# GRU and mixture-of-experts kernel: input projections begun ahead of the recurrence, preparation in another order, five low halves on GpSimd

## The chip, the cores and the metric

The kernel runs on one core of one Trainium2 chip. The metric is the device time of an execution in microseconds. The kernel before has a median of 913.2 us over 3 runs (912.21 to 913.89). TensorE, VectorE, ScalarE, GpSimd and SyncE run side by side, each through its own instructions in order, and wait for each other by semaphores. The profile calls them PE (matmuls) with PEld (weight loads), DVE, ACT, POOL and SP.

## The reference

A GRU is scanned over 128 time steps of 16 sequences of width 512 (here 4 batches of 512 tokens, laid out so that the kernel can treat them as blocks), and its states go through a layer of four experts of which each token takes two; the result is added to x. Cut to what matters:

```python
def cell(h, x):
    gi = x @ W_ih + b_ih
    gh = h @ W_hh + b_hh
    i_r, i_z, i_n = jnp.split(gi, 3, axis=-1)
    h_r, h_z, h_n = jnp.split(gh, 3, axis=-1)
    r = sigmoid(i_r + h_r); z = sigmoid(i_z + h_z)
    n = tanh(i_n + r * h_n)
    return (1 - z) * n + z * h
_, hs = lax.scan(cell, cond_2048, x)           # x: 4 x 512 tokens of width 512
logits = hs @ Wg + bg                          # 4 experts, top 2, softmax
for i in range(4):                             # each takes its 512 best tokens
    out[sel] += gelu(tok @ W1[i]) @ W2[i] * p
x + out
```

## The kernel before

The sequences are cut into 64 columns that are computed side by side. A run of 40 steps over these columns follows: `FIRST` = 24 steps that bring the start states near their values (the first `ROUGH` = 20 of them with 16-bit high halves of the state alone), then 16 steps whose states are kept. After that come the gate of the experts, the choice of tokens, and for each expert two products (L538 and L551).

**The input projection gi = x W_ih** (12 tiles of 128 outputs by 512 columns, for each of four chunks of x) is made in two ways. The first chunk's 12 tiles are 32-bit matmuls on TensorE (L351), made before the recurrence. A tile lands in one of four banks of PSUM (banks 4 to 7). ScalarE scales and keeps it (`keep_tile`, L594: L601 for the r and z gates' tiles 0 to 7, L604 for the n gate's tiles 8 to 11), writes the high half in 16 bits (L616, `rz_high`), and VectorE subtracts to get the low half (L965, `rz_low`). An r or z tile stays in a ring of three buffers `gi_full` (`GI_RING`, L53), so that tile t can be kept only when the low half of tile t-3 is made (semaphore `gi_low`, L600). The other three chunks are made of 16-bit products, 12 matmuls a tile, 432 in all (`fill`, L355, matmul L368). They are given out over the first 24 steps of the recurrence, 18 a step (`FILL_STEP`), in a rough step as 13, 2, 2 and 1 ahead of the four parts of the state product (L376); ScalarE keeps these tiles behind a step's own work and VectorE makes their two halves at its end (`between`, L1135: a cast L958 and a subtraction L965).

**Chunk borders.** At steps 8 and 16 TensorE waits for all r, z high halves of the chunk that begins (L398), at step 24 for all high and low halves (L435, L436). TensorE's injection of gi into the gates is L386.

**The preparation** also takes the largest absolute value of x, W_ih, W_hh on VectorE (L919, L923, L931, L985, L1009), has GpSimd spread each over the partitions (`partition_all_reduce`: L768, L771, L774), turns it into powers of two, and splits W_ih, W_hh and x into halves (ScalarE L580, L584, L591; VectorE L973, L979). GpSimd then does one tiny product (L777, `warm`), and from then on the products z h of each step (L786).

SyncE issues all large loads, x of the first chunk first (L287), then W_ih in thirds (L289), the next x, W_hh in four parts, the rest of x. The order of work on each engine is written out by hand.

Of the kernel before, what the change touches and what calls it, by code (L numbers as in the profile page):

```python
# [36 lines left out]
def gru_moe(nc, x, x_t, cond_t, w_ih, w_hh, b_ih, b_hh, wg, bg, w1, w2, hs_rows, out):  # L37
# [18 lines left out]
    with ExitStack() as ctx:  # L56
# [154 lines left out]
        S["wih_loaded"] = [sem(f"wih_loaded_{g}") for g in range(3)]  # L211
        S["whh_loaded"] = [sem(f"whh_loaded_{k}") for k in range(KD)]
# [32 lines left out]
        assert FILL_STEP * STEPS_C == GI_MMS  # L245
# [13 lines left out]

        def rz_count(t):  # L260

            return sum(m < 8 for _, m in TILES[:t])

        def split_by(i):

            return 12 + 3 * (i + (i % STEPS_C == STEPS_C - 1)) // 2
# [19 lines left out]
        def _(sp):  # L286
            sp.dma_start(x_first, x_t[:, CHUNK_ORDER[0], :, :]).then_inc(S["x_loaded"][0], 16)  # L287
            for g in range(3):
# [48 lines left out]
        def _(pe):  # L337

            def bank_free(t):

                if t >= 4:
                    pe.wait_ge(S["gi_kept"], t - 3)

            pe.wait_ge(S["x_loaded"][0], 16)
            for m in range(12):
# [4 lines left out]
                for k in range(KD):  # L350
                    mm = pe.matmul(ps[:, 4 + m % 4, :], wih_sb[:, k, m * P:(m + 1) * P], x_first[:, k, :],  # L351
# [3 lines left out]
            def fill(first, last):  # L355

                for n in range(first, last):
# [10 lines left out]
                    mm = pe.matmul(ps[:, 4 + tile % 4, :], wih_parts[:, w, k, m * P:(m + 1) * P],  # L368
# [24 lines left out]
            def gates_rough(src, i):  # L393
                n = FILL_STEP * i
# [28 lines left out]

            pe.wait_ge(S["diag_ready"], 1)
            pe.wait_ge(S["whh_high"], KD)
            for i in range(ROUGH):
                gates_rough(i % 2, i)
            pe.wait_ge(S["whh_ready"], WHH_PIECES)
            for i in range(ROUGH, FIRST + L):
                if i < FILLED:  # L430
                    fill(FILL_STEP * i, FILL_STEP * i + FILL_STEP)
# [41 lines left out]
            pe.wait_ge(S["turn_ready"], 1)  # L473
# [91 lines left out]
        def _(act):  # L565
# [28 lines left out]
            def keep_tile(t, q, sc, g_sc):  # L594
# [3 lines left out]
                if m < 8:  # L598
                    if rz_count(t) >= GI_RING:
                        act.wait_ge(S["gi_low"], rz_count(t) - GI_RING + 1)  # L600
                    act.activation(gi_full[:, rz_count(t) % GI_RING, :], ps[:, 4 + t % 4, :], ACT.Identity,  # L601
                                   bias=bias_gi[:, q, m:m + 1], scale=sc).then_inc(S["gi_kept"], 1)
                else:
                    act.activation(gi[:, c, m % 4, 2, :], ps[:, 4 + t % 4, :], ACT.Identity, bias=bsum_g[:, m:m + 1],  # L604
# [19 lines left out]
            for m in range(4):  # L624
                first_tile(m)
            wih_high(0)
            wih_high(1)
            first_tile(4)
            wih_high(2)
            first_tile(5)  # L630
            wih_high(3)
            for k in range(KD):
                x_high(0, k)
            first_tile(6)
            act.wait_ge(S["gates_known"], 1)
            whh_high(0)
            first_tile(7)
            whh_high(1)
            whh_high(2)
            first_tile(8)  # L640
# [815 lines left out]
```

## Time and profile before

| | us |
|---|---|
| median of 3 runs | 913.2 |
| the profiled execution | 913.26 |
| its span, first to last instruction | 911.5 |
| first rough step's gates begin | 65.7 |
| PE busy, share of the span | 810.2 (89%) |
| DVE busy | 634.6 (70%) |
| ACT busy | 414.3 (45%) |
| POOL busy | 178.2 (20%) |

Times inside the profile count from the span's start. A row of a timeline gives start, duration, engine, line, what it writes and reads, its shape, how many are merged, and in brackets how long its engine had been idle and what ended that. Rows of one engine overlap by some 0.05 to 0.1 us, so that the distance between starts is a little under the duration. The granted clock of TensorE is given as a share of its 2.4 GHz.

### The profile page before, as it was taken

The page shows a single profiled execution, that of the slowest core. Times are in us where ns is not written, and L with a number is a line of the kernel's source. Part 1 is how long each engine was busy: PE and PEld are TensorE (multiplying, and loading weights), DVE is VectorE, ACT ScalarE, POOL GpSimd, SP SyncE. Part 2 cuts the span into 40 slices and gives each one's busy share as a digit, 9 for nine tenths or more (in the row PEclk, how much of TensorE's full clock was granted, in tenths as well). Part 3 has the DMA queues.
Part 4 walks back from the last instruction along what each step waited for, and adds up shares of the span by engine and source line. Part 5 has one row for each costly group of instructions (what it writes and reads, how often), then busy time and mean ns, then how long its engine had stood idle before and what let it go on. Part 6 is the DMA issues. An engine that isn't in the chain of part 4 may idle for free.

```text
span 911.5 us, 28124 instructions
## 1 busy us (share of the span) xinstructions
PE 810.2 (89%) x11698; PEld 533.4 (59%) x11699; DVE 634.6 (70%) x2087; ACT 414.3 (45%) x852; POOL 178.2 (20%) x454
## 2 busy tenths in 40 slices
PE   5979899997999999999957145999999999999996
PEld 2436565576999899999947143444444444444442
DVE  6868989765888888888875666766775766774500
ACT  0747566543454454545434302834283347416600
POOL 1002212122333333433320001012102100110011
PEclk9989999998999999999987557999999999999999
DMA  9800000000000000000013561247143715360011
GB/s 343 304 0 2 2 1 3 2 3 3 4 5 4 4 4 5 4 4 4 4 29 160 147 223 47 97 136 208 24 138 94 212 16 186 69 193 12 1 24 23
DMA packets 20165, 62.57 MB, mean 69 GB/s; under 512 B 2064, under 2 KB 2064, under 8 KB 17424
## 3 DMA queue, kind: packets, MB, share of 16 engines
q1 hardware_dynamic: 15744, 52.46, 16.6%
q0 software_dynamic: 3584, 8.42, 5.2%
q8 instruction: 85, 1.39, 0.6%
q14 instruction: 32, 0.26, 0.1%
q10 hardware_dynamic: 720, 0.03, 0.1%
HBM read 52.49 MB, written 12.62 MB: 71 GB/s over the span
## 4 chain that ended last, share of the span: by engine, by line
PE 69%; DVE 20%; issue 4%; ACT 3%; DMA 1%; POOL 0%; DVEq 0%; ACTq 0%; POOLq 0%
PE ps L376 18%; PE ps L538 18%; PE ps L551 18%; PE ps L368 8%; DVE wa L1047 4%; DVE wa L1052 3%; DVE halves L1063 3%; ACT wa L648 2%; PE ps L480 2%; PE ps L386 2%; DVE ocand L1056 1%; PE ps L518 1%; PE ps L526 1%; DMA bg_sb<-in_bg 1%; DVE big L965 1%
## 5 line engine op out<-in xcount | busy, mean ns | idle before, releaser
L376 PE MATMUL ps<-halves,wa 128*128 128x64 f16 x8448 | 290.6, 194 | 7.9 <-DVE halves L1063 1.6
L376 PEld LDWEIGHTS ps<-halves,wa 128*128 128x128 f16 x8448 | 274.2, 98 | 35.4 <-DVE halves L1063 15.9
L538 PE MATMUL ps<-wb,big 128*128 128x512 f16 x768 | 166.9, 379 | 1.5 <-DVE wb L1351 1.5
L551 PE MATMUL ps<-big 128*128 128x512 f16 x768 | 166.9, 379 | 0.0
L648 ACT ACTIVATE wa<-ps,un_gates 128x128 f32<-128x128 f32 x288 | 100.1, 365 | 139.0 <-PE ps L376 132.5
L1047 DVE SCALAR_TENSOR_TENSOR wa<-ps,bhn_s,wa 128x64 f32<-128x64 f32 x288 | 80.2, 278 | 72.2 <-ACT wa L648 72.2
L538 PEld LDWEIGHTS ps<-wb,big 128*128 128x128 f16 x768 | 74.7, 98 | 91.5 <-issue 1.7
L551 PEld LDWEIGHTS ps<-big 128*128 128x128 f16 x768 | 75.2, 98 | 89.9
L653 ACT ACTIVATE wa<-wa,un_gates 128x64 f32<-128x64 f32 x288 | 99.1, 344 | 57.5 <-DVE wa L1052 51.1
L368 PE MATMUL ps<-hx,wb 128*128 128x512 f16 x432 | 109.7, 386 | 4.9 <-DVEq L1022 4.9
L713 ACT ACTIVATE hx<-ps,un_hid_in 128x512 f32<-128x512 f32 x64 | 43.7, 683 | 112.4 <-PE ps L538 112.4
L1063 DVE SCALAR_TENSOR_TENSOR halves<-ocand,neg_scale,wa 128x64 f16<-128x64 f32 (+1 forms) x288 | 86.8, 301 | 4.5 <-issue 0.5
L1243 DVE SCALAR_TENSOR_TENSOR big<-wa,scale,big 128x2048 f16<-128x2048 f32 x28 | 65.3, 2349 | 26.0 <-ACT big L699 26.0
L699 ACT ACTIVATE big<-wa,scale 128x2048 f16<-128x2048 f32 x32 | 62.5, 1988 | 44.6 <-DVEq L1231 44.6
L1364 DVE SCALAR_TENSOR_TENSOR big<-hx,hid_scale,big 128x512 f16<-128x512 f32 x64 | 47.9, 749 | 42.8 <-ACT big L716 41.4
L386 PE MATMUL ps<-big,diag 128*128 128x128 f16 x496 | 62.8, 221 | 10.9 <-DVE big L958 10.9
L1202 DVE TENSOR_REDUCE chunk_peak<-wa 128x1 f32<-128x2048 f32 x32 | 71.1, 2276 | 0.0
L1052 DVE TENSOR_TENSOR wa<-wa,big 128x64 f32<-128x64 f32 x288 | 66.0, 229 | 5.1
L1056 DVE SCALAR_TENSOR_TENSOR ocand<-wa 128x64 f32<-128x64 f32 x288 | 62.6, 217 | 0.1
L368 PEld LDWEIGHTS ps<-hx,wb 128*128 128x128 f16 x432 | 38.5, 99 | 40.8 <-DVEq L1022 5.7
L786 POOL TENSOR_TENSOR wa<-wa,hx 128x64 f32<-128x64 f32 x128 | 42.6, 333 | 78.7 <-ACT wa L648 73.9
L844 POOL DMA_INDIRECT out<-hx,idx_out x16 | 29.1, 1816 | 136.1 <-DVE hx L1370 136.1
(178 smaller groups left out, 686.2 us busy)
## 6 DMA issues: line engine op xcount, KB each, us to landing
wa<-in_w SPq DMA_DIRECT2D x32, 1024.0 KB, 5.9
hs_rows<-big SPq DMA_DIRECT2D x8, 516.0 KB, 6.2
big<-in_w_ih SPq DMA_DIRECT2D x3, 1024.0 KB, 11.4
hx<-in_x_t SPq DMA_DIRECT2D x3, 1024.0 KB, 20.2
big<-in_w_hh SPq DMA_DIRECT2D x4, 768.0 KB, 16.5
wa<-in_x_t SPq DMA_DIRECT2D x1, 1024.0 KB, 5.2
hx<-hs_rows,idx POOLq DMA_INDIRECT x16, 3.7
out<-hx,idx_out POOLq DMA_INDIRECT x16, 4.8
```

What stands on the lines that cost most here:

```text
L368: mm = pe.matmul(ps[:, 4 + tile % 4, :], wih_parts[:, w, k, m * P:(m + 1) * P], x_parts[:, q, t, k, :], start=(left == 0), stop=(left == K ...
L376: mm = pe.matmul(gate_ps[:, j, g, :], whh_parts[:, k, w, (4 * g + j) * P:(4 * g + j + 1) * P], halves[:, src, k, h, :], start=False, stop= ...
L386: pe.matmul(gate_ps[:, j, 0:2, :], diag[:, 1 if c in (1, 2) else 0, :], gi_rz[:, c, j, part, :, cols], start=(part == HIGH), stop=False, s ...
L538: mm = pe.matmul(ps[:, m % 2, :], w1p[:, w, k, m * P:(m + 1) * P], tokT[:, t, k, :], start=(k == 0 and n == 0), stop=(k == KD - 1 and n == 2))
L551: mm = pe.matmul(ps[:, 2 + g % 2, :], hid[:, h, k, g * P:(g + 1) * P], w2p[:, w, k, :], start=(k == 0 and n == 0), stop=(k == KH - 1 and n ...
L648: act.activation(rz[:, j, :, :], gate_ps[:, j, 0:2, :], ACT.Sigmoid, scale=un_gates[:, 0:1]).then_inc(S["sig_done"], 1)
L653: act.activation(cand[:, j, :], cand_in[:, j, :], ACT.Tanh, scale=un_gates[:, 0:1]).then_inc(S["tanh_done"], 1)
L1047: dve.scalar_tensor_tensor(rn[:, j, :], gate_ps[:, j, 2, :], bhn_s[:, j:j + 1], rz[:, j, 0, :], ALU.add, ALU.mult).then_inc(S["rn_done"], 1)
L1052: dve.tensor_tensor(cand_in[:, j, :], rn[:, j, :], gi_n(j), ALU.add).then_inc(S["candin_ready"], 1)
L1056: dve.scalar_tensor_tensor(ocand[:, j, :], rz[:, j, 1, :], -1.0, cand[:, j, :], ALU.add, ALU.mult).then_inc(S["ocand_done"], 1)
L1063: dve.scalar_tensor_tensor(high_of(j), old(ocand_, j), neg_scale[:, 0:1], old(zh_, j), ALU.mult, ALU.add).then_inc(S["high_ready"], 1)
L1202: dve.tensor_reduce(chunk_peak[:, c:c + 1], stage[:, c * CHUNK:(c + 1) * CHUNK], AX.X, ALU.max, apply_absolute_value=True).then_inc(S["chu ...
```

## The change

Five things are edited.

- **Fills ahead.** The first 24 of the 432 fill matmuls (`PREFILL`, two tiles) are issued before the recurrence; the steps then take 18 each from number 24 on, until all are given out, so that step 22 has 12 and step 23 none. ScalarE keeps a tile once the first 13 fills of the next step can have made it (`kept_by`), and VectorE makes the halves one step later (`split_by`).
- **Banks.** The first chunk's 12 tiles use all eight banks (`gi_bank`), so TensorE waits for a kept tile only from tile 8 on. As the recurrence uses banks 0 to 3, TensorE waits for `gi_kept` 12 before its first step.
- **Loads.** x of the first chunk and the first third of W_ih come in four pairs of pieces, and the first four tiles are made piece by piece.
- **Order.** VectorE takes the biases after the maxima, takes the four maxima of W_hh in a row, and moves the splits of W_ih and x behind the scales of the gates; ScalarE keeps three tiles, splits W_ih and x, and then alternates the other r, z tiles with W_hh.
- **GpSimd.** It makes the four copies of the identity into `turn` (as products) and the low halves of tiles 3 to 7. These stand behind its three `partition_all_reduce` and the `warm` product, and wait for `gi_low` 3, that is for VectorE's low halves of tiles 0 to 2.

GpSimd's order in the preparation, before (`peak_all` is what it spreads, `warm` the tiny product, `ISA` rows without a tile carry no data):

```order
L768 ISA
L768 ISA peak_all<-peak 128x3 [waits peak_ready]
L771 ISA peak_all<-peak 128x2 [waits peak_ready]
L774 ISA peak_all<-peak 128x1 [waits peak_ready]
L777 ISA
L777 TENSOR_TENSOR warm<-ones 128x1 [waits consts_dve]
L786 TENSOR_TENSOR wa<-wa,halves 128x64 [waits sig_done] x80
```

The same place after (`big<-gi_full,big` are the low halves):

```order
L795 ISA
L795 ISA peak_all<-peak 128x3 [waits peak_ready]
L798 ISA peak_all<-peak 128x2 [waits peak_ready]
L801 ISA peak_all<-peak 128x1 [waits peak_ready]
L804 ISA
L804 TENSOR_TENSOR warm<-ones 128x1 [waits consts_dve]
L806 TENSOR_TENSOR turn<-ident 128x128 x4
L810 TENSOR_TENSOR big<-gi_full,big 128x512 [waits gi_high,gi_low]
L810 TENSOR_TENSOR big<-gi_full,big 128x512 [waits gi_high] x4
L821 TENSOR_TENSOR wa<-wa,halves 128x64 [waits sig_done] x80
```

Nine products now stand between `warm` and the first product of the recurrence.

ScalarE's order from the first tile that needs GpSimd's low halves to the recurrence, after (L627 keeps a tile in the ring, L642 writes its high half, L610 is W_hh's high half, L630 keeps an n tile):

```order
L610 ACTIVATE wa<-big,scale 128x1536 [waits gates_known]
L627 ACTIVATE gi_full<-ps,bias_gi,gi_scale 128x512 [waits gi_low,gi_mm]
L642 ACTIVATE big<-gi_full 128x512 [waits gi_kept]
L610 ACTIVATE wa<-big,scale 128x1536
L627 ACTIVATE gi_full<-ps,bias_gi,gi_scale 128x512 [waits gi_low,gi_mm]
L642 ACTIVATE big<-gi_full 128x512 [waits gi_kept]
L610 ACTIVATE wa<-big,scale 128x1536
L627 ACTIVATE gi_full<-ps,bias_gi,gi_scale 128x512 [waits gi_low,gi_mm]
L642 ACTIVATE big<-gi_full 128x512 [waits gi_kept]
L610 ACTIVATE wa<-big,scale 128x1536
L630 ACTIVATE big<-ps,bsum_g,gates_scale 128x512 [waits gi_mm] x4
```

These are tiles 5, 6 and 7, each followed by a part of W_hh, and then the four n tiles; before, tile 6 stood ahead of the first part of W_hh and tile 7 behind it.

TensorE at the start of the recurrence, after:

```order
L392 MATMUL ps<-hx,wb 128x512 [waits gi_kept,x_split,wih_split]
L392 MATMUL ps<-hx,wb 128x512 x11
L392 MATMUL ps<-hx,wb 128x512 [waits gi_kept]
L392 MATMUL ps<-hx,wb 128x512 x11
L392 MATMUL ps<-hx,wb 128x512 [waits gi_kept,whh_high,diag_ready]
L392 MATMUL ps<-hx,wb 128x512 x11
L392 MATMUL ps<-hx,wb 128x512 [waits gi_kept]
L410 MATMUL ps<-big,diag 128x128 [waits rn_done,high_ready,gi_high]
```

Two tiles of 12 fills stand ahead of the wait for W_hh and `diag`, where before there was none.

The diff, without the parts in which only a bank's name changes:

```diff
S["wih_loaded"] = [sem(f"wih_loaded_{g}") for g in range(3)]
+        S["first_loaded"] = [sem(f"first_loaded_{k}") for k in range(KD)]
         S["whh_loaded"] = [sem(f"whh_loaded_{k}") for k in range(KD)]
...
         GI_MMS = 12 * KD * 3
-        assert FILL_STEP * STEPS_C == GI_MMS
+        PREFILL = 24
+        assert FILL_STEP * STEPS_C == GI_MMS and PREFILL % (3 * KD) == 0
+
+        def filled(i):
+
+            return min(PREFILL + FILL_STEP * i, 3 * GI_MMS)
...
+        def gi_bank(t):
+
+            return t % 8 if t < 12 else 4 + t % 4
+
         def rz_count(t):
...
+        def kept_by(i):
+
+            return 12 + (PREFILL if i < 0 else min(filled(i) + FILLS[0], 3 * GI_MMS)) // (3 * KD)
+
         def split_by(i):
-            return 12 + 3 * (i + (i % STEPS_C == STEPS_C - 1)) // 2
+            return kept_by(i - 1) if i >= 0 else 12
+        assert split_by(STEPS_C - 1) >= 24 and split_by(2 * STEPS_C - 1) >= 36 and split_by(FILLED - 1) == 48
+        assert kept_by(2 * STEPS_C - 1) <= 38
...
         def _(sp):
-            sp.dma_start(x_first, x_t[:, CHUNK_ORDER[0], :, :]).then_inc(S["x_loaded"][0], 16)
-            for g in range(3):
+            for k in range(KD):
+                sp.dma_start(x_first[:, k, :], x_t[:, CHUNK_ORDER[0], k, :]).then_inc(S["first_loaded"][k], 16)
+                sp.dma_start(wih_sb[:, k, 0:D], wih_src[:, k, 0:D]).then_inc(S["first_loaded"][k], 16)
+            for g in range(1, 3):
                 sp.dma_start(wih_sb[:, :, g * D:(g + 1) * D], wih_src[:, :, g * D:(g + 1) * D]
...
-                if t >= 4:
-                    pe.wait_ge(S["gi_kept"], t - 3)
-
-            pe.wait_ge(S["x_loaded"][0], 16)
-            for m in range(12):
+                if t >= 8:
+                    pe.wait_ge(S["gi_kept"], t - 7 if t < 16 else t - 3)
+
+            for k in range(KD):
+                pe.wait_ge(S["first_loaded"][k], 32)
+                for m in range(4):
+                    mm = pe.matmul(ps[:, gi_bank(m), :], wih_sb[:, k, m * P:(m + 1) * P], x_first[:, k, :],
+                                   start=(k == 0), stop=(k == KD - 1))
+                    if k == KD - 1:
+                        mm.then_inc(S["gi_mm"], 1)
+            for m in range(4, 12):
...
                 for k in range(KD):
-                    mm = pe.matmul(ps[:, 4 + m % 4, :], wih_sb[:, k, m * P:(m + 1) * P], x_first[:, k, :],
+                    mm = pe.matmul(ps[:, gi_bank(m), :], wih_sb[:, k, m * P:(m + 1) * P], x_first[:, k, :],
                                    start=(k == 0), stop=(k == KD - 1))
...
                         bank_free(tile)
-                    mm = pe.matmul(ps[:, 4 + tile % 4, :], wih_parts[:, w, k, m * P:(m + 1) * P],
+                    mm = pe.matmul(ps[:, gi_bank(tile), :], wih_parts[:, w, k, m * P:(m + 1) * P],
                                    x_parts[:, q, t, k, :], start=(left == 0), stop=(left == KD * 3 - 1))
...
             def gates_rough(src, i):
-                n = FILL_STEP * i
+                n = filled(i)
                 for k in range(KD):
...
+            fill(0, PREFILL)
             pe.wait_ge(S["diag_ready"], 1)
             pe.wait_ge(S["whh_high"], KD)
+            pe.wait_ge(S["gi_kept"], 12)
             for i in range(ROUGH):
...
                 if i < FILLED:
-                    fill(FILL_STEP * i, FILL_STEP * i + FILL_STEP)
+                    fill(filled(i), filled(i + 1))
                 if i == ROUGH:
...
-            pe.wait_ge(S["turn_ready"], 1)
+            pe.wait_ge(S["turn_ready"], KD + 1)
             for n in range(NT):
...
                         act.wait_ge(S["gi_low"], rz_count(t) - GI_RING + 1)
                                    bias=bias_gi[:, q, m:m + 1], scale=sc).then_inc(S["gi_kept"], 1)
                 else:
                                    scale=g_sc).then_inc(S["gi_kept"], 1)
...
             act.wait_ge(S["x_known"], 1)
-            for m in range(4):
+            for m in range(3):
                 first_tile(m)
-            wih_high(0)
-            wih_high(1)
-            first_tile(4)
-            wih_high(2)
-            first_tile(5)
-            wih_high(3)
+            for k in range(KD):
+                wih_high(k)
+            act.wait_ge(S["x_loaded"][1], 16)
             for k in range(KD):
                 x_high(0, k)
-            first_tile(6)
+            first_tile(3)
+            first_tile(4)
             act.wait_ge(S["gates_known"], 1)
             whh_high(0)
+            first_tile(5)
+            whh_high(1)
+            first_tile(6)
+            whh_high(2)
             first_tile(7)
-            whh_high(1)
-            whh_high(2)
-            first_tile(8)
             whh_high(3)
-            for m in range(9, 12):
+            for m in range(8, 12):
                 first_tile(m)
...
             act.wait_ge(S["gi_known"], 1)
+            for t in range(12, kept_by(-1)):
+                tile(t)
             for i in range(FIRST + L):
...
                     continue
-                for t in range(12 + 3 * i // 2, 12 + 3 * (i + 1) // 2):
+                for t in range(kept_by(i - 1), kept_by(i)):
                     tile(t)
...
             pool.tensor_tensor(warm[:, :], ones[:, 0:1], ones[:, 0:1], ALU.mult).then_inc(S["warmed"], 1)
+            for k in range(KD):
+                pool.tensor_tensor(turn[:, k, 0:P], ident[:, :], ident[:, :], ALU.mult).then_inc(S["turn_ready"], 1)
+            pool.wait_ge(S["gi_low"], 3)
+            for t in range(3, 8):
+                pool.wait_ge(S["gi_high"], t + 1)
+                pool.tensor_tensor(gi_rz[:, CHUNK_ORDER[0], t % 4, LOW, t // 4, :], gi_full[:, t % GI_RING, :],
+                                   gi_rz[:, CHUNK_ORDER[0], t % 4, HIGH, t // 4, :], ALU.subtract
+                                   ).then_inc(S["gi_low"], 1)
...
             dve.wait_ge(S["steps_made"], 1)
-            dve.wait_ge(S["small_loaded"], 16 * 5)
-            dve.tensor_tensor(bsum[:, 0:8], bih[:, 0:8], bhh[:, 0:8], ALU.add)
-            dve.tensor_copy(bsum[:, 8:12], bih[:, 8:12]).then_inc(S["bias_ready"], 1)
-            dve.wait_ge(S["bias_ready"], 1)
-            dve.tensor_reduce(peak[:, BIAS:BIAS + 1], bsum[:, 0:8], AX.X, ALU.max, apply_absolute_value=True)
...
-            dve.wait_ge(S["x_loaded"][0], 16)
+            for k in range(KD):
+                dve.wait_ge(S["first_loaded"][k], 32)
             dve.tensor_reduce(chunk_peak[:, 3:4], x_first, AX.XY, ALU.max, apply_absolute_value=True
...
             for g in range(3):
-                dve.wait_ge(S["wih_loaded"][g], 16)
+                if g > 0:
+                    dve.wait_ge(S["wih_loaded"][g], 16)
                 dve.tensor_reduce(chunk_peak[:, g:g + 1], wih_sb[:, :, g * D:(g + 1) * D], AX.XY, ALU.max,
...
             link_n[0] += 4
-            dve.wait_ge(S["consts_pool"], 1)
-            for k in range(KD):
-                dve.tensor_copy(turn[:, k, 0:P], ident[:, :])
+            dve.wait_ge(S["small_loaded"], 16 * 5)
+            dve.tensor_tensor(bsum[:, 0:8], bih[:, 0:8], bhh[:, 0:8], ALU.add)
+            dve.tensor_copy(bsum[:, 8:12], bih[:, 8:12]).then_inc(S["bias_ready"], 1)
+            dve.wait_ge(S["bias_ready"], 1)
+            dve.tensor_reduce(peak[:, BIAS:BIAS + 1], bsum[:, 0:8], AX.X, ALU.max, apply_absolute_value=True)
             dve.tensor_copy(turn[:, :, P:P + E], wg_sb[:, :, :]).then_inc(S["turn_ready"], 1)
...
-            for m in range(4):
-                rz_low(m)
-
             def wih_low(k):
...
                 ins = dve.tensor_reduce(chunk_peak[:, k:k + 1], whh_sb[:, k, :], AX.X, ALU.max, apply_absolute_value=True)
-                if k < KD - 1:
-                    wih_low(k)
-                if k in (1, 2):
-                    rz_low(3 + k)
             link(ins)
...
             dve.sem_inc(S["peak_ready"], 1)
-            wih_low(KD - 1)
-            rz_low(6)
+            rz_low(0)
+            dve.wait_ge(S["consts_pool"], 1)
             dve.wait_ge(S["peak_known"], 2)
...
             dve.sem_inc(S["gates_known"], 1)
-            for k in range(KD):
-                x_low((0, k))
-            rz_low(7)
+            wih_low(0)
+            rz_low(1)
             for n in range(2, NC_):
...
             dve.sem_inc(S["peak_ready"], 1)
+            wih_low(1)
+            rz_low(2)
+            wih_low(2)
+            wih_low(3)
+            for k in range(KD):
+                x_low((0, k))
             dve.wait_ge(S["peak_known"], 3)
...
             dve.sem_inc(S["gi_known"], 1)
+            dve.wait_ge(S["gi_low"], 8)
...
```

## Rows read from the trace of the kernel before

**Rows 1.** Timeline of the preparation, VectorE (columns as told above).
```profile
11.43 0.17 DVE L893 TENSOR_TENSOR bsum<-bih,bhh 128x8 f32<-128x8 f32 x1 [7.58 <-DMA bg_sb<-in_bg]
...
20.56 0.62 DVE L928 COPY turn<-ident 128x128 f32<-128x128 f32 x4
...
32.50 1.75 DVE L985 TENSOR_REDUCE chunk_peak<-big 128x1 f32<-128x1536 f32 x1
...
34.16 1.81 DVE L973 SCALAR_TENSOR_TENSOR wb<-big,scale,wb 128x1536 f16<-128x1536 f32 x1
...
48.48 0.16 DVE L909 TENSOR_SCALAR peak_all<-peak_all 128x2 f32<-128x2 f32 x1
...
53.48 4.41 DVE L1009 TENSOR_REDUCE peak<-hx 128x1 f32<-128x4096 f32 x1
```
**Rows 2.** Timeline of the preparation, TensorE.
```profile
9.70 15.99 PE L351 MATMUL ps<-wa,big 128*128 128x512 f32 x32 [9.70 <-DMA big<-in_w_ih]
...
60.85 5.00 PE L368 MATMUL ps<-hx,wb 128*128 128x512 f16 x13 [4.92 <-DVEq L1022]
```
**Rows 3.** Timeline of the preparation, GpSimd.
```profile
11.69 0.28 POOL L736 TENSOR_SCALAR_AFFINE_SELECT ident<-ident 128x128 f32<-128x128 f32 x1 [10.71 <-issue]
...
14.66 0.22 POOL L764 TENSOR_SCALAR_AFFINE_SELECT earlier<-earlier 128x16 f32<-128x16 f32 x1
23.91 0.39 POOL L768 PARTITION_ALL_REDUCE peak_all<-peak  x1 [9.02 <-DVEq L934]
...
58.04 0.37 POOL L774 PARTITION_ALL_REDUCE peak_all<-peak  x1 [11.52 <-DVEq L1011]
66.03 0.18 POOL L777 TENSOR_TENSOR warm<-ones 128x1 f32<-128x1 f32 x1 [7.62 <-issue]
```
**Rows 4.** Timeline of the preparation, ScalarE.
```profile
26.44 0.78 ACT L601 ACTIVATE gi_full<-ps,bias_gi,gi_scale 128x512 f32<-128x512 f32 x1 [20.93 <-DVEq L952]
...
49.93 1.58 ACT L584 ACTIVATE wa<-big,scale 128x1536 f16<-128x1536 f32 x1 [5.78 <-DVEq L1003]
51.41 0.76 ACT L601 ACTIVATE gi_full<-ps,bias_gi,gi_scale 128x512 f32<-128x512 f32 x1
...
52.74 3.03 ACT L584 ACTIVATE wa<-big,scale 128x1536 f16<-128x1536 f32 x2
...
57.80 2.10 ACT L604 ACTIVATE big<-ps,bsum_g,gates_scale 128x512 f32<-128x512 f32 x3
```
**Rows 5.** GpSimd's products, from the groups with shapes kept apart.
```profile
L786 POOL TENSOR_TENSOR wa<-wa,hx 128x64 f32<-128x64 f32 x128 | 42.6, 333 | 78.7 <-ACT wa L648 73.9
```
**Rows 6.** Two rough steps of TensorE, timeline.
```profile
150.40 2.97 PE L368 MATMUL ps<-hx,wb 128*128 128x512 f16 x13
155.91 2.97 PE L368 MATMUL ps<-hx,wb 128*128 128x512 f16 x13
```
**Rows 7.** Chain that ended last (start, us, what), borders at steps 8, 16.
```profile
112.21 0.69 DVE big L965
...
113.30 0.29 PE ps L386
...
120.32 0.06 PE ps L386
...
161.28 0.23 PE ps L386
```
**Rows 8.** The same chain: an exact step with fills, two starts without.
```profile
189.21 3.88 PE ps L368 x18
...
233.61 1.97 PE ps L376 x63
238.70 2.12 PE ps L376 x63
```
**Rows 9.** Windows: length, then busy of PE, PEld, DVE, ACT, POOL, granted clock, DMA.
```profile
210.16:219.96 9.80, 4.65 (x153) 4.55 (x150) 6.43 (x27) 3.86 (x10) 1.94 (x6) 0.93 0.01 3
219.96:225.30 5.34, 5.34 (x93) 5.34 (x94) 0.00 (x0) 0.00 (x0) 0.00 (x0) 0.50 0.01 3
```

More of the change, by code:

```diff
@@ L600, in keep_tile @@
                         act.wait_ge(S["gi_low"], rz_count(t) - GI_RING + 1)
-                    act.activation(gi_full[:, rz_count(t) % GI_RING, :], ps[:, 4 + t % 4, :], ACT.Identity,
+                    act.activation(gi_full[:, rz_count(t) % GI_RING, :], ps[:, gi_bank(t), :], ACT.Identity,
                                    bias=bias_gi[:, q, m:m + 1], scale=sc).then_inc(S["gi_kept"], 1)
                 else:
-                    act.activation(gi[:, c, m % 4, 2, :], ps[:, 4 + t % 4, :], ACT.Identity, bias=bsum_g[:, m:m + 1],
+                    act.activation(gi[:, c, m % 4, 2, :], ps[:, gi_bank(t), :], ACT.Identity, bias=bsum_g[:, m:m + 1],
                                    scale=g_sc).then_inc(S["gi_kept"], 1)
```

## The prediction

> **What bounds the kernel now.** I read the page's shares first, then the chain that ended last, then each engine's timeline over the preparation. TensorE is busy for most of the span, and the change touches only what lies ahead of the last 16 steps, so three stretches count.
>
> The preparation lasts until TensorE's first 13 fills at 60.85 us. TensorE had been idle for 4.92 us there and waited for VectorE's last scale [rows 2]. VectorE works almost without a gap up to it, but it begins late: it sat 7.58 us until small loads came in at 11.43, although the first x and first third of W_ih were there at 9.70, when TensorE started [rows 1, 2]. GpSimd has long idle stretches with one of a special kind: 7.62 us ahead of `warm`, ended by nothing but its own issue, directly behind a `partition_all_reduce` (58.04 + 0.37 to 66.03) [rows 3]. The ISA row between the two in its order is what stands there. Another such stretch, 10.71 us, ends at 11.69. I read both as GpSimd changing its code. In the kernel before the one of 7.62 us hid nothing but `warm`.
>
> In a rough step TensorE is the bound: 13 fills follow 13 fills at 5.51 us without a hole [rows 6]. At the borders VectorE is: the chain goes over its low halves at 112.21 to the injection at 113.30 (step 8), and the same at 161.28 (step 16) [rows 7]. In exact steps with fills TensorE is again the bound (3.88 us are 18 fills); without them a step takes 5.09 us, of which TensorE works 4.65 [rows 8, 9].
>
> **The preparation, step by step.** VectorE no longer waits for the small loads and starts its maxima at about 9.7; the biases' small work goes behind them, and the four `turn` copies (0.62) leave: its first peaks are ready some 2.2 us earlier, at about 21.7 instead of 23.9 [rows 1, 3]. But GpSimd must load the code of its reduction behind L764, which ends at 14.88. No row shows that load alone; the bounds are the 7.62 of the other change and the 9.02 that lay between. I take 7.62: the reduction runs at 22.5, 1.4 us earlier than 23.91, not 2.2. (With 9.02 nothing is gained.) ScalarE then starts at 25.0 instead of 26.44, VectorE is free at 24.8.
>
> From there VectorE: four W_hh maxima at 1.66 (32.50 to 34.16), 31.5; two short links and low half 0, 1.1, 32.6; scales of the gates 1.45 (48.48 to 49.93), 34.0; the low part of W_ih 1.73 and low half 1 0.6, 36.4; maximum of the last x 4.41, 40.8 [rows 1, 4]. GpSimd reduces it by 41.3, against 58.41 before. Then it changes code: 7.62, to 48.9. All five low halves of GpSimd are behind this in program order, though their data (`gi_low` 3) is there at 43.1 (40.8, a part of W_ih 1.73, low half 2 0.6).
>
> Its products: 64 columns take 333 ns, `warm` with one column 183 [rows 3, 5]. The slope, 2.4 ns a column, gives 0.49 us for 128 columns (0.45 from start to start) and 1.4 us for 512. Bounds: 0.69, VectorE's own time for the low half [rows 7], and 2.7, eight times the row of 64 columns. So `warm` 0.15, four copies 1.8, low half of tile 3 1.4: 52.3. The Trainium skill (GPSIMD Engine Reference, 3.1) has 4497 ns for a two-input product of 2048 columns, twice VectorE's time. By it a low half of 512 would be an estimated 1.1 to 1.3 us, and the sum 0.2 us less. The same page (2.1, Instruction dispatch) says that the first call of a freshly loaded kernel pays about 6 us of code load with no instruction in the profile. The trace has the same thing at 7.62; by 6 us both changes would be 1.6 shorter and the forecast 3 us lower.
>
> ScalarE waits for that low half with tile 6: the ring of three wants `gi_low` 4. It has nothing else to do from 46.1 on: tile 5 needs low half 2 at 43.1, tile and W_hh part take 1.33 + 1.48, with 0.2 between. Queued behind are tile 6, a part of W_hh, tile 7, the last part, four n tiles: 1.33 + 1.48 + 1.33 + 1.48 + 2.75 = 8.4 us (51.41 to 52.74; 49.93 to 51.41; 2.10 for three n tiles) [rows 4]. That is 60.7. Tile 7 wants the low half of tile 4, ready at 53.7, in time. TensorE waits for all of it: it has ended the first chunk at about 49 (12 tiles at 16 us a four, started near 5.5, the slower first passes in the first four [rows 2]), makes the 24 fills (0.216 each [rows 8], 5.2) by 54.7 after `x_split` at 49.5 (43.1, two parts of W_ih 3.5, four of x at 0.7 by their size), and then waits for `gi_kept` 12 until 60.7, six idle microseconds. The 13 fills before took 5.00 us behind 4.92 of idleness, at half clock, where 2.97 is normal [rows 2, 6]; I take the same. The gates begin at 65.7, where they began before. **The preparation gains 0.0.** Five low halves taken off VectorE (3.0 us) buy nothing, since the change of code has taken the place of VectorE's chain.
>
> **The recurrence.** Rough steps are the same 18 fills and stay at 5.51. VectorE's work between steps is one tile's two halves and a split, below its free time, as before; step 0 has two tiles, 2.1 us, and about 2 free.
>
> Border at step 8: step 7 has one r, z tile to halve and not two, and the wait is over 1.04 us earlier (0.69 + 0.35) [rows 7]. From injection to injection step 8 took 7.02 us (113.30 to 120.32) where 5.51 is normal [rows 6, 7]: behind 3.5 us of idle TensorE. The idleness falls to 2.4, like that ahead of 161.28 (155.91 + 2.97 = 158.88), after which the clock had not fallen. So 1.5 more. Border at 16: 1.04.
>
> Steps 22 and 23 lose 6 and 18 fills. 24 fills at 0.216 are 5.2; less the hole of 5.09 - 4.65 = 0.44 that opens: 4.7 [rows 8, 9]. Border at 24: one tile less, 1.04, less 0.3 because VectorE is late out of the shorter step 22: 0.7.
>
> Sum: 0.0 + 2.5 + 1.0 + 4.7 + 0.7 = 9.0. The profiled execution has 913.26, the median is 913.2, 0.06 apart. **Forecast 904.2 us.** All behind the recurrence moves with it.
>
> **Rivals.**
> *Code changes cost nothing here*: if the 7.62 us are not paid again between reduction and product, GpSimd's first low half is ready at 44.7, ScalarE ends at 54.4, TensorE has 24 fills done at 54.7 without idleness and takes 2.8 for the next 13 at 2.4 GHz: gates at 57.5, 8.2 earlier, 896.0. For it: GpSimd moves no data there. Against: the order keeps the ISA row between the same two. 10%.
> *Slower loads of code*: 9.02 for the first and the 10.71 of 11.69 for the second [rows 3], since x is being copied to the output at that time: 1.4 + 3.1, 908.7. 12%.
> *The clock holds at step 24*: TensorE idles 4.4 instead of 5.2 there; before, the granted clock was 0.50 (1.2 GHz) from 219.96 to 225.30, and from the injection to the first sigmoid took 5.3 where the step before took 2.8 [rows 9]. 2.5 less, 901.7. 13%.
> *The shorter last steps give nothing*, VectorE's chain being the bound there: 4.7 less, 908.9. Against it the holes of 0.44. 5%.
> *Slower than before*: GpSimd's low halves at a price p each. VectorE waits for all five before its first step, which it wants at 68.9; they end at 50.9 + 5 p. From p = 3.6 on each us costs five, from 5.4 on the 9.0 are lost; at 6 the kernel takes 916. The rows give 1.4. The Trainium skill (GPSIMD Engine Reference, 4.1 Engine selection) sends elementwise work to VectorE, GpSimd being some two times slower for two inputs; that speaks for this side, but its factor, 1.4 against VectorE's 0.69, would not reach it. 3%.
>
> **How the numbers follow.** The forecast's own case (gates within a microsecond or two of 65.7, gains in the steps as summed) has 55%, from 902 to 907; 2% is for what I don't see. A difference of 0.2%, 1.8 us, is what a measurement can tell. Within it (911.4 to 915.0) only mishaps of slow loads and lost steps together land, 3%; slower is 3% + 1%; faster the rest, 93%. The range goes from 897 to 909, which leaves out the first rival and the slow side.
>
> **What would show it.** In the profile after: GpSimd idle some 7.6 us for "issue" ahead of its tiny product, near 41 to 49; ScalarE idle about six before tile 6, ended by GpSimd's low half; GpSimd's low halves near 1.4 each; TensorE idle about six ahead of the third tile of fills and those at half clock; first injection at 65 to 66; step 8's injection 1.0 earlier against step 7 and its clock full; no fills in step 23 and exact steps of 5.1 from there. The forecast is wrong if the tiny product runs right behind the reduction (896), or if the first injection comes after 69.

## The result, and the profile after

The changed kernel takes 908.58 us (median of 5 runs, 908.1 to 909.42) against 913.2 (5 runs): a ratio of 0.9946, 95% interval 0.9932 to 0.9961. That is faster, inside the range, and 4.4 us above the forecast of 904.2. Its profiled execution took 908.32, with a span of 906.6 against 911.5.

GpSimd's timeline in the preparation of the changed kernel answers to [rows 3]:

```profile
23.54 0.39 POOL L795 PARTITION_ALL_REDUCE peak_all<-peak  x1 [10.40 <-DVEq L968]
33.25 0.92 POOL L798 PARTITION_ALL_REDUCE peak_all<-peak  x1 [9.33 <-DVEq L1020]
42.72 0.37 POOL L801 PARTITION_ALL_REDUCE peak_all<-peak  x1 [8.55 <-DVEq L1037]
51.89 0.18 POOL L804 TENSOR_TENSOR warm<-ones 128x1 f32<-128x1 f32 x1 [8.80 <-issue]
52.05 1.47 POOL L806 TENSOR_TENSOR turn<-ident 128x128 f32<-128x128 f32 x4
53.48 4.48 POOL L810 TENSOR_TENSOR big<-gi_full,big 128x512 f16<-128x512 f32 x4
```

The stretch ended by nothing but "issue" is there again, 8.80 us, and now five low halves and four copies stand behind it. The chain that ended last now goes through it (start, us, what):

```profile
42.72 0.37 POOL peak_all L801
43.09 0.06 POOLq L804 x2
43.15 8.74 issue
51.89 0.18 POOL warm L804
52.07 1.44 POOL turn L806 x4
53.51 1.13 POOL big L810
...
54.72 0.79 ACT gi_full L627
...
60.42 2.68 ACT big L630 x4
...
63.34 2.72 PE ps L392 x6
```

One low half on GpSimd takes 1.13 us, then the chain crosses to ScalarE's tile 6, which had waited for it, and follows its queue to the four n tiles:

```profile
54.72 0.78 ACT L627 ACTIVATE gi_full<-ps,bias_gi,gi_scale 128x512 f32<-128x512 f32 x1 [6.56 <-POOL big L810]
```

VectorE and TensorE in the same stretch, answering to [rows 1, 2]:

```profile
11.60 2.29 DVE L950 TENSOR_REDUCE chunk_peak<-wa 128x1 f32<-128x2048 f32 x1 [7.74 <-DMA big<-in_w_ih]
...
53.22 1.49 DVE L1052 TENSOR_SCALAR diag<-ident,un_gi 128x128 bf16<-128x128 f32 x2
```

```profile
4.41 16.43 PE L365 MATMUL ps<-wa,big 128*128 128x512 f32 x32 [4.41 <-DMA big<-in_w_ih]
20.68 27.63 PE L375 MATMUL ps<-wa,big 128*128 128x512 f32 x64
51.36 5.34 PE L392 MATMUL ps<-hx,wb 128*128 128x512 f16 x24 [3.05 <-issue]
63.34 4.94 PE L392 MATMUL ps<-hx,wb 128*128 128x512 f16 x13 [6.64 <-ACT big L630]
```

TensorE begins 5.3 us earlier and still ends up idle for 6.64 us, waiting for ScalarE. The gates begin at 68.12, 2.4 later than before. The windows from there on (length, busy of PE, PEld, DVE, ACT, POOL, granted clock, DMA) go from injection to injection at steps 0, 8, 9, 16, 22 and 24:

```profile
68.12:114.47 46.35, 44.23 (x562) 26.94 (x560) 38.80 (x153) 29.36 (x79) 9.90 (x32) 1.00 0.01 2
114.47:121.78 7.31, 7.31 (x75) 4.45 (x76) 4.49 (x16) 2.26 (x8) 1.14 (x4) 0.77 0.01 2
121.78:161.66 39.88, 38.55 (x491) 23.41 (x488) 36.80 (x141) 27.67 (x73) 8.46 (x28) 1.00 0.01 2
161.66:200.71 39.05, 39.05 (x622) 26.40 (x623) 28.92 (x125) 20.68 (x57) 9.11 (x30) 1.00 0.01 2
200.71:214.86 14.15, 9.59 (x305) 9.22 (x302) 11.97 (x53) 6.48 (x18) 4.01 (x12) 0.97 0.01 3
```

| stretch | before | after | difference | forecast |
|---|---|---|---|---|
| to the first injection | 65.7 | 68.1 | +2.4 | 0.0 |
| steps 0 to 7 and the border at 8 | 47.6 | 46.35 | -1.3 | -1.0 |
| step 8 | 7.0 | 7.3 | +0.3 | -1.5 |
| steps 9 to 15 and the border at 16 | 41.0 | 39.9 | -1.1 | -1.0 |
| steps 16 to 23 and the border at 24 | 58.7 | 53.2 | -5.5 | -5.4 |
| the rest of the span | 691.5 | 691.7 | +0.2 | 0.0 |

The rest hides two differences. From its injection to the next one step 24 took 5.87 us (214.86 to 220.73), before 7.11 (219.96 to 227.07), and in the experts' part that was lost again: the changed kernel reaches the matmuls of L552 at 549.84, 7.0 us ahead of the kernel before (L526, 556.86), and is 4.9 ahead at the end.

### The profile page after: what moved, and what is told of

The parts are those of the page before. It is cut to its first block, busy times and chain, and to the rows that moved or that the text cites. A ratio compares the mean times of both kernels' runs of the same rounds, so it can differ in the third digit from the quotient of the medians.

```text
span 906.6 us, 28131 instructions
## 1 busy us (share of the span) xinstructions
PE 810.2 (89%) x11698; PEld 531.2 (59%) x11699; DVE 631.3 (70%) x2078; ACT 414.3 (46%) x852; POOL 185.8 (20%) x463
## 4 chain that ended last, share of the span: by engine, by line
PE 68%; DVE 19%; issue 6%; ACT 3%; DMA 1%; POOL 1%; DVEq 0%; SPq 0%; POOLq 0%; ACTq 0%
PE ps L564 19%; PE ps L577 18%; PE ps L400 18%; PE ps L392 8%; DVE wa L1080 4%; DVE wa L1085 3%; DVE halves L1096 3%; ACT wa L673 2%; PE ps L410 2%; PE ps L506 2%; DVE ocand L1089 1%; PE ps L552 1%; PE ps L544 1%; DMA big<-in_w_ih 1%; DVE chunk_peak L1016 1%
## 5 line engine op out<-in xcount | busy, mean ns | idle before, releaser
L564 PE MATMUL ps<-wb,big 128*128 128x512 f16 x768 | 168.8, 382 | 1.5 <-DVE wb L1384 1.5
```

The lines of the kernel that those rows point to most:

```text
L564: mm = pe.matmul(ps[:, m % 2, :], w1p[:, w, k, m * P:(m + 1) * P], tokT[:, t, k, :], start=(k == 0 and n == 0), stop=(k == KD - 1 and n == 2))
```

## The experiments

All were timed beside the kernel before, whose medians in the three calls were 914.1, 913.3 and 914.9 us.

**e1: all low halves on VectorE.**

```diff
-            for t in range(3, 8): ... pool.tensor_tensor(... subtract)
+            wih_low(2); rz_low(3); rz_low(4); wih_low(3); x_low x4; rz_low(5)
+            ... gi_scales(1); rz_low(6) ... diag; rz_low(7)
```

> All eight low halves of the first chunk on VectorE; GpSimd keeps the four copies into turn. Theory A (GpSimd's change of code, 8.8 us behind its third reduction, sets the end of the preparation, since tile 6 waits for a low half behind it): ScalarE no longer waits 6.6 us ahead of tile 6, TensorE idles under 1 us ahead of the third tile of fills, the first injection comes at 60 to 62 instead of 68.1, the kernel takes 901 to 903. Theory B (VectorE's chain and ScalarE's order set it, and GpSimd's wait only stands in front of work that would be late anyway): five low halves of 0.6 more on VectorE make it 3 us longer, the injection comes at 68 to 71, 909 to 912.

902.16 us (900.58 to 902.64), ratio 0.9864 (0.9843 to 0.9884): theory A. GpSimd's change of code is still there, but no one waits for it:

```profile
51.33 1.47 POOL L804 TENSOR_TENSOR warm<-ones 128x1 f32<-128x1 f32 x1 [8.58 <-issue]
52.76 1.47 POOL L806 TENSOR_TENSOR turn<-ident 128x128 f32<-128x128 f32 x4
```

```profile
52.23 9.83 PE L392 MATMUL ps<-hx,wb 128*128 128x512 f16 x37 [4.47 <-issue]
61.90 0.22 PE L410 MATMUL ps<-big,diag 128*128 128x128 f16 x1
```

TensorE runs its 24 and 13 fills in one piece and injects at 61.90, 6.2 us before the changed kernel, with 3 us more work on VectorE. At step 8 its clock stayed at full, which gave this trace 1.6 us more.

**e2: the new preparation without fills ahead.**

```diff
-        PREFILL = 24
+        PREFILL = 0
(kept_by and split_by by the formulas of before)
```

> The new preparation without fills ahead: all 432 fills in 24 steps of 18, tiles kept and split by the rules of the kernel before. Theory A: the preparation costs 2.4 us by itself (first injection at 68.1 against 65.7) and the recurrence gains nothing: 915 to 916. Theory B (the 24 fills ahead are what makes the preparation late): the injection returns to about 65.7, 913.2.

916.88 us (12 runs, 915.58 to 920.69), ratio 1.0031 (1.0014 to 1.0047): alone, the preparation makes the kernel slower, by 0.3%. Its injection came at 69.27. Theory B is out: the 24 fills do not make the preparation late. That it came out a little above 916 goes with VectorE's first maximum, which began at 12.90 in this trace, 1.3 later than in the changed kernel.

**e3: the fills ahead in the old preparation.**

```diff
(kernel before, with PREFILL, filled, kept_by and split_by of the change, and)
+            fill(0, PREFILL)
             pe.wait_ge(S["diag_ready"], 1)
...
             act.wait_ge(S["gi_known"], 1)
+            for t in range(12, kept_by(-1)):
+                tile(t)
```

> The kernel before with the 24 fills ahead and the new rules of keeping and splitting, nothing else. Theory A: TensorE's 24 fills run from about 56 to 61 without idleness before them, the next 13 at full clock, first injection near 64; with about 7 us from the steps the kernel takes 903 to 906 and is faster than the whole change. Theory B (the gain in the steps needs the new preparation, or 24 fills in the old one push everything back by 5.2 us): 907 or more.

903.54 us (903.28 to 903.72), ratio 0.9878 (0.9858 to 0.9899): this one part beats the whole change by 5 us.

```profile
56.66 8.15 PE L376 MATMUL ps<-hx,wb 128*128 128x512 f16 x37 [0.65 <-ACT big L613]
64.64 0.22 PE L394 MATMUL ps<-big,diag 128*128 128x128 f16 x1
```

The fills take the place of the old 4.92 us of idleness [rows 2], and so the 13 that follow run at full clock: the injection is 1.0 earlier than before although 5.2 us of work were put ahead of it. Of the 5 us on the changed kernel 3.5 stand at the first injection and 1.6 at step 8, where the clock held (5.51 us against 7.14).

**e4: the first loads whole.**

```diff
-            for k in range(KD): (x_first[:, k], wih_sb[:, k, 0:D] one by one)
+            sp.dma_start(x_first, ...); sp.dma_start(wih_sb[:, :, 0:D], ...)
```

> The change with the first x in one load and the first third of W_ih in one, as before; TensorE and VectorE wait for both. Theory A (the eight pieces arrive 1.9 us later than two whole loads, 11.6 against 9.7, and VectorE starts late by that): VectorE's first maximum at 9.7, the first reduction on GpSimd 1 to 1.9 earlier (it also waits for its code), injection at 66.2 to 67.1, 906.7 to 907.6. Theory B (the pieces cost nothing, VectorE waits for the same bytes): nothing within 0.5 us of 908.6.

908.44 us (906.34 to 909.71), ratio 0.9926 (0.9905 to 0.9947). The total does not tell the theories apart; the trace does:

```profile
9.80 2.29 DVE L949 TENSOR_REDUCE chunk_peak<-wa 128x1 f32<-128x2048 f32 x1 [5.96 <-DMA big<-in_w_ih]
```

```profile
21.74 0.39 POOL L795 PARTITION_ALL_REDUCE peak_all<-peak  x1 [7.74 <-DVEq L967]
...
50.69 0.19 POOL L804 TENSOR_TENSOR warm<-ones 128x1 f32<-128x1 f32 x1 [9.39 <-issue]
```

VectorE starts 1.8 us earlier, as A has it, and all of that arrives at the first reduction, so GpSimd's first load of code fits into 7.74 us. At the third reduction 1.8 are still there (40.92 against 42.72). Then the change of code takes 9.39 and swallows 0.6 of them. The injection comes at 66.33, 1.8 earlier again: TensorE was idle for 3.77 us and not 6.64 ahead of the last 13 fills, and they took 0.6 less. Of this gain 1.2 were lost at step 24 (7.04 us against 5.87). Between 4 and 8 us the loads ran at 192 GB/s in pieces and 383 GB/s whole; the whole ones had such a slow stretch too, 192 GB/s, but from 8 to 10.

**e5: the last two reductions of GpSimd together.**

```diff
             rz_low(0)
+            (maximum of the last x, peak_ready 3); rz_low(1); rz_low(2)
             dve.wait_ge(S["peak_known"], 2)
```

> The change with VectorE's maximum of the last x moved ahead of the scales of the gates (and low halves 0 to 2 in a row behind it), so that GpSimd's second and third reduction stand together and its change of code begins at about 38.8 instead of 43.1; GpSimd still makes the five low halves. Theory A (the change of code sets the end of the preparation): tile 6 is kept 4.3 us earlier, at about 50.4, the first injection comes at 62 to 64, the kernel takes 902 to 904.5. Theory B (VectorE's chain sets it, and that has the same work in another order): injection within 0.5 us of 68.1, 908.6.

908.27 us (906.74 to 910.8), ratio 0.9942 (0.9918 to 0.9966). My number was wrong by 4 us:

```profile
38.01 0.92 POOL L801 PARTITION_ALL_REDUCE peak_all<-peak  x1 [4.25 <-DVEq L1026]
50.31 0.18 POOL L804 TENSOR_TENSOR warm<-ones 128x1 f32<-128x1 f32 x1 [11.38 <-issue]
```

The change began 4.2 us earlier and ended 1.6 earlier; it took 11.38 us. Between the two reductions, which now follow each other, there is no such stretch: the 4.25 us end with VectorE's maximum. Theory B does not follow, since the injection moved with the end of the change (66.24, 1.9 earlier). What stretched it is the question of e9.

**e6: two more changes of code, no more work.**

```diff
             pool.partition_all_reduce(peak_all[:, 0:2], ...)
+            pool.tensor_tensor(warm[:, :], ...)
             pool.wait_ge(S["peak_ready"], 3)
             pool.partition_all_reduce(peak_all[:, X1:X1 + 1], ...)
-            pool.tensor_tensor(warm[:, :], ...)
```

> The change with the tiny product moved between GpSimd's second and third reduction, so that GpSimd changes its code three times behind the second reduction and not once; no work is added. Theory A (each change between product and reduction costs 7.6 us or more): the third reduction runs near 51 instead of 42.7, the copies begin near 60, tile 6 waits until 62 to 64, the injection comes at 75 to 78, the kernel takes 916 to 919. Theory B (the stretch of 8.8 us is a single cost, for instance of the first product or of loads that run at that time): the third reduction within 1 us of 42.7 and the kernel within 1 us of 908.6.

916.65 us in a single run, so it is read from its trace: theory A. Tile 6 waited until 63.31, the injection came at 76.44, 8.3 us later than in the changed kernel for two more changes.

```profile
45.97 1.29 POOL L801 TENSOR_TENSOR warm<-ones 128x1 f32<-128x1 f32 x1 [11.47 <-issue]
53.24 0.38 POOL L803 PARTITION_ALL_REDUCE peak_all<-peak  x1 [5.98 <-issue]
60.64 1.46 POOL L806 TENSOR_TENSOR turn<-ident 128x128 f32<-128x128 f32 x4 [7.02 <-issue]
```

Each swap between a reduction and a product pays, in both directions: 11.47 to the product, 5.98 to the reduction, 7.02 to the products.

**e7: low halves on VectorE and whole loads.** The edits of e1 and e4 together.

```diff
-            for k in range(KD): (x_first[:, k], wih_sb[:, k, 0:D] one by one)
+            sp.dma_start(x_first, ...); sp.dma_start(wih_sb[:, :, 0:D], ...)
-            for t in range(3, 8): ... pool.tensor_tensor(... subtract)
+            rz_low(3); rz_low(4); ... rz_low(5); ... rz_low(6); ... rz_low(7)
```

> All low halves on VectorE as in e1, and the first loads whole as in e4: meant as the better version. Theory: VectorE begins at 9.8 and ends its splits 1.4 us earlier than in e1; TensorE starts at 9.75 and then is the bound itself, 12 tiles to 53.1, 24 fills to 58.4 and 13 more at full clock, first injection at 61.2 against 61.9 in e1: 901 to 902, no more than 1 us better than e1. A rival in which VectorE alone set the end in e1 would have the injection at 60.4 and 900.5.

899.32 us (898.63 to 900.92), ratio 0.9837 (0.9807 to 0.9868), 9 us better than the change. The injection at 61.02 is the theory's 61.2, with TensorE in one piece:

```profile
25.57 27.63 PE L375 MATMUL ps<-wa,big 128*128 128x512 f32 x64
53.04 8.15 PE L392 MATMUL ps<-hx,wb 128*128 128x512 f16 x37
61.02 0.22 PE L410 MATMUL ps<-big,diag 128*128 128x128 f16 x1
```

The total is 2 us better than I wrote; TensorE's clock held at full from there to step 24, past step 8, which my number had not counted on.

**e8: four buffers in the ring.**

```diff
-    GI_RING = 3
+    GI_RING = 4
```

> The change with four buffers in the ring of kept tiles and not three; no instruction is added or moved. Theory A (GpSimd's low halves reach ScalarE through the ring): tile 6 no longer waits for GpSimd, being let in by VectorE's low half 2 at 45, and tile 7 waits for the low half of tile 3 at 54.6, so ScalarE's queue behind it is shorter by a tile and a part of W_hh: everything 2.8 to 2.9 us earlier, injection at 64.5 to 65.5, 905 to 906. Theory B (the wait at the ring is no part of the chain that ends the preparation): within 0.5 us of 908.6.

903.36 us (901.8 to 905.74), ratio 0.9884 (0.985 to 0.9918): A, and more than its number. Not one instruction moves, and the wait moves from tile 6 to tile 7 (ScalarE's only wait for GpSimd):

```profile
53.88 0.78 ACT L627 ACTIVATE gi_full<-ps,bias_gi,gi_scale 128x512 f32<-128x512 f32 x1 [5.77 <-POOL big L810]
```

ScalarE ends 3.6 us earlier. The shorter queue accounts for 2.8 of them, as written; the other 0.8 came from the change of code, which took 8.04 us here and 8.80 in the changed kernel, though the two kernels are the same up to there. After 1.53 us of idleness and not 6.64, TensorE makes the 13 fills at full clock, 2.0 us shorter:

```profile
59.71 2.97 PE L392 MATMUL ps<-hx,wb 128*128 128x512 f16 x13 [1.53 <-ACT big L630]
62.52 0.22 PE L410 MATMUL ps<-big,diag 128*128 128x128 f16 x1
```

The injection comes 5.6 us before the changed kernel's.

**e9: e5 with the copy of x to the output held back.**

```diff
             sp.wait_ge(S["x_loaded"][NC_ - 1], 16)
+            sp.wait_ge(S["warmed"], 1)
             sp.dma_start(out..., x...)
```

> e5 (both last reductions of GpSimd together) with the copy of x to the output held back until GpSimd's tiny product is done. In e5 the change of code took 11.4 us, from 38.9 to 50.3, where 7.6 was read before. Theory A (GpSimd's code comes by memory traffic and is slowed by the copy that runs from about 31 to 44): the change takes 7.6 to 8, to about 46.7; tile 6 is kept near 50, the first injection comes at 60.5 to 62.5, the kernel takes 900.5 to 903. Theory B (the time of the change hangs on when it begins, or on VectorE's splits, which run in both): 11 to 11.5 us again, the kernel within 1 us of e5's 908.3.

906.85 us (904.29 to 907.69), ratio 0.9913 (0.9893 to 0.9932).

```profile
38.29 0.92 POOL L802 PARTITION_ALL_REDUCE peak_all<-peak  x1 [4.25 <-DVEq L1027]
46.16 0.20 POOL L805 TENSOR_TENSOR warm<-ones 128x1 f32<-128x1 f32 x1 [6.95 <-issue]
46.33 4.39 POOL L807 TENSOR_TENSOR turn<-ident 128x128 f32<-128x128 f32 x4
```

On the disputed point A is right: begun at the same time as in e5, the change takes 6.95 us and not 11.38, with the copy out of the way. The total fell short of my number, because three of the four us were lost again one row later: the four copies took 4.39 us where they took 1.47. They now lie beside VectorE's splits of W_ih and x, which read two tensors. The held copy ran at that time too, from 46.45, so e9 alone does not separate the two; but in e1 and e7, with no transfer under way, GpSimd's work was also slow beside such splits (`warm` 1.47 us in place of 0.18, the four copies 2.60). The injection came at 63.80.

**e10: low halves on VectorE, first loads in halves.**

```diff
(e1, and)
-            for k in range(KD): (x_first[:, k], wih_sb[:, k, 0:D] one by one)
+            for k in range(0, KD, 2): (x_first[:, k:k + 2], wih_sb[:, k:k + 2, 0:D])
```

> All low halves on VectorE, and the first loads in two pairs of halves instead of four pairs of quarters or two whole ones: meant as the best version. Theory (more pieces arrive later as a whole, fewer let TensorE start later): TensorE starts near 6.5, VectorE near 10.3, the first chunk ends at 50.5, VectorE's splits at 51, 24 fills by 56.3 and 13 more at full clock, injection at 59 to 60, 898 to 899, 1 us better than whole loads. Rival (the halves arrive as late as the quarters): VectorE at 11.3, injection at 60.5 to 62, 900 to 902.

899.12 us (898.02 to 904.9), ratio 0.9833 (0.9808 to 0.9859). TensorE began at 6.16, VectorE at 10.45, the injection came at 59.41, 8.7 us before the changed kernel: the theory's numbers. The total is the same as e7's, and not 1 us better: the injection is 1.6 earlier, but here the clock was at half for 3.4 us at step 8 and there it was not.

## Why the prediction was right, and where its sizes were off

*The outcome.* The direction was right and the time lies in the range of 897 to 909, but by 0.4 us only: the gain was 4.6 us where 9.0 were forecast, and 908.58 is outside the 902 to 907 that I gave my own case. That it stands next to the 908.7 of the rival with slow loads of code is chance; the terms below are others.

*What bounds the preparation.* Right, and shown three ways: e1 takes the low halves off GpSimd, e8 moves the wait without moving an instruction, e6 adds changes of code. The chain after runs through the row of 8.74 us of issue. The rival in which a change of code costs nothing (896) is out by e6; 61.90 and 61.02 in e1 and e7 are what the preparation gives when no one waits for GpSimd. The rival of slow loads of code was true in part: the second change took 8.80 and not the rival's 10.71, and the first load of code was not even 7.62, since in e10 the reduction ran 7.28 us behind GpSimd's work ahead of it, and still waited for VectorE.

*The term that failed is the preparation's 0.0; it measured +2.4.* Its parts: VectorE's first maximum stood at 9.7 in my sum and began at 11.60, as the eight pieces arrive later than two loads (e4: 9.80). I had taken the whole loads' landing for the pieces'. In my sum GpSimd's first load of code (7.62) hid part of such a delay, so that it cost 1.0 at the first reduction (23.54 against 22.5). The stretch from there to the end of the third reduction was 0.75 longer than summed; the second reduction took 0.92, where the others in [rows 3] took 0.37 to 0.39, and VectorE waited 0.34 for it. The change of code took 8.80 and not 7.62, +1.2. Against these, GpSimd's copies and low half were cheaper than the slope gave (1.44 and 1.13 against 1.8 and 1.4), -0.6. ScalarE's queue (8.4) and the 13 fills at half clock (4.8 against 5.0) were as summed. The end of the first chunk was right too (48.3 against 49), though not by "16 us a four": only the first four tiles take 16, the other eight 27.63.

*Step 8's clock: forecast -1.5, measured +0.3.* The border came 1.3 us earlier, 1.0 were summed, but the shorter idleness did not protect the clock: the window shows 0.77 granted. Before and after:

```profile
113.30 0.29 PE L386 MATMUL ps<-big,diag 128*128 128x128 f16 x1 [3.38 <-DVE big L958]
114.47 0.23 PE L410 MATMUL ps<-big,diag 128*128 128x128 f16 x1 [2.12 <-DVE big L992]
```

That the step became longer than before has to do with when the clock fell: before, the first matmul behind the idleness was slow already (0.29 against 0.23), so that a part of the time at 1.2 GHz fell on the idleness; after, all 3.4 us fell on work. I had drawn a line from one case (2.4 idle ahead of 161.28, full clock) and one of 3.5. The runs show no such line: of the ten traces with one tile less at this border (the changed kernel and all but e2) seven have TensorE at 1.2 GHz for 3.4 us there, and e1, e3 and e7 don't. The idleness ahead was 2.11 to 2.48 us in all ten, and the longest, 2.48, stands in e1, where the clock held, and in e4, where it did not. What decides is open. In e3 the clock is 1.00 over step 8, which took 5.51 us (to 116.50), and the start of step 9:

```profile
110.99:118.00 7.01, 7.01 (x101) 4.61 (x102) 5.57 (x21) 3.59 (x10) 1.14 (x4) 1.00 0.01 2
```

The gain to be had was also a little less than 1.5: the row at 120.32 is a later matmul of step 9's injection, which began at 120.16, so that step 8 took 6.86 before (7.14 after, by the same reading).

*The rival of the clock at step 24* came half true: the window from 214.86 to 220.73 has 0.77 granted where 219.96 to 227.07 has 0.62. That, too, changes from trace to trace: the step took 6.00 in e3 and 7.0 to 7.4 in e1, e2, e4, e5 and e7 to e10.

*The steps.* Right in place and size: -1.3, -1.1 and -5.5 against -1.0, -1.0 and -5.4. Steps 22 and 23 lose what their fills cost less the hole of 0.44 (58.7 to 53.2), so TensorE was the bound there; the rival in which they give nothing is out.

*The slow side.* GpSimd's low halves cost 1.13 each, far from the 5.4 at which they would have decided. As a whole, though, moving them was the wrong way round: the change is 6.4 us slower than e1, which differs only in who makes them. It is faster than before only because the fills ahead (9.7 us alone by the medians 913.2 and 903.54, 10.6 by the 914.1 beside it) outweigh a preparation that loses (e2). What loses in it are GpSimd's low halves; with them on VectorE it adds to the fills (e7, 899.32, against e3, 903.54).

The Trainium skill (GPSIMD Engine Reference, 2.1 Instruction dispatch) gives about 6 us for the code load behind a fresh kernel, with nothing to see in the profile. The traces agree on the second half: the row says only "issue", and in e9 no transfer shows in the whole stretch (39.21 to 46.16), so that it is a load of code rests on this page; the runs show that it comes with each swap between the two kinds. Its times are 6.95 to 7.79 with memory quiet and up to 11.47 beside the copy; the one in the other direction was 5.98. The Trainium skill (GPSIMD Engine Reference, 3.1 Elementwise) has 4497 ns for 2048 columns; the estimate from it, 1.1 to 1.3 us a low half, was nearer to the measured 1.13 than my slope from 64 columns, 1.4.

## What to carry to other kernels

An engine that looks idle may not be free: before work is moved to it, read what ends its long idle stretches, and where the answer is "issue" between two kinds of instruction, the work will queue behind that stretch in program order, however early its data is. Look also at who frees the buffers of a small ring: one more buffer (e8) made the kernel 5 us faster here, as much as the whole change, though only 2.8 of it were the shorter queue; the rest were TensorE's clock and a shorter change of code. And time the parts of a change alone; here one part gained twice what the whole did.

## What the runs showed of the hardware

- GpSimd's change of code from `partition_all_reduce` to elementwise products: 7.62 and 7.79 us begun at 58 and 7.02 begun at 53.6 (e6), with no large transfer under way; 8.04 to 9.39 begun at 41 to 44, when the copy of x to the output was ending; 11.38 and 11.47 begun at 39 and 34.5, with that copy (4 MB within memory) under way until 43 and 44; 6.95 begun at 39 without it. The copy is what stretches it (e5 against e9, which differ in nothing else). From product to reduction it was 5.98. One reduction behind another has no such stretch (4.25 us in e5, ended by VectorE).
- GpSimd and VectorE were slower side by side. GpSimd's product of 128 columns took 0.37 us in the changed kernel and 1.1 beside VectorE's splits (e9, where a copy in memory ran too); in e1 `warm` took 1.47 and not 0.18 beside such a split, with no transfer. VectorE's two `diag` products took 0.48 us in e1 and 1.49 in the changed kernel, where GpSimd's low halves ran beside them.
- Eight loads of 256 KB in place of two of 1 MB brought TensorE's start from 9.7 to 4.4, and VectorE's first maximum, which waits for the last piece, from 9.80 and 9.97 to between 11.17 and 12.90.
- TensorE's clock fell to 1.2 GHz for 3.4 us behind 2.1 to 2.5 us of idleness in seven traces, and did not in three.
